# A Mamba mixer with an FP4 FFN on one core: state tiles of four states by 32 channels with quadrant sums, tanh silu, preparation a turn ahead, delta*x through two DRAM buffers

## The reference

```
xs, z = split(x @ in_w)                       # 512 channels each
xc    = silu(cb + sum_k shift(xs, k) * cw[k]) # 4 taps
dt, B, C = split(xc @ xp_w)                   # 16, 16, 16
delta = softplus(dt @ dt_w + dt_b);  A = -exp(A_log)
h[t]  = h[t-1] * exp(delta[t]*A) + (delta[t]*xc[t]) * B[t]   # 512 channels x 16 states
y[t]  = sum_n h[t,:,n] * C[t,n] + xc[t] * D
x     = layer_norm((y * silu(z)) @ out_w + x)
```

## Time and profile before

| | us |
|---|---|
| median of three runs (12323.26 to 12326.33) | 12323.49 |
| the profiled execution's own time | 12305.88 |
| its span, first to last instruction | 12304.1 |
| from the first scan to the last one's end | 11013.3 |
| the same for one of 64 turns | 172.1 |

### The profile page before, as it was taken

One profiled execution on the slowest core, in us unless ns is written; L12 is line 12 of the kernel. 1 busy time (PEld: TensorE's weight loads), 2 busy tenths in 40 slices (PEclk: granted clock), 3 DMA queues, 4 the chain that ended last, 5 costly groups with the idle time before them and its releaser, 6 DMA issues. The chain is left out here.

```text
span 12304.1 us, 107024 instructions
## 1 busy us (share of the span) xinstructions
PE 8618.5 (70%) x20260; PEld 3527.3 (29%) x20260; DVE 11095.7 (90%) x14024; ACT 4922.0 (40%) x6934; POOL 7372.0 (60%) x5182
## 2 busy tenths in 40 slices
PE   4767777777777777777777777777777777775566
PEld 1222222222222222222222222222222222222344
DVE  7999999999999999999999999999999999996555
ACT  3434443444434443444444443444344443442222
...
GB/s 91 34 38 36 38 21 38 37 43 28 34 38 36 38 21 38 38 41 31 31 38 36 38 25 35 37 43 31 31 38 36 38 25 35 38 35 25 25 25 23
DMA packets 191635, 433.27 MB, mean 35 GB/s; under 512 B 10928, under 2 KB 155056, under 8 KB 157552
## 3 DMA queue, kind: packets, MB, share of 16 engines
q1 hardware_dynamic: 190960, 427.63, 9.8%
...
## 5 line engine op out<-in xcount | busy, mean ns | idle before, releaser
L632 POOL TENSOR_TENSOR hc<-h,c_all 128x512 f32<-128x512 f32 x4096 | 5833.3, 1426 | 3959.7 <-DVE h L711 2933.5
L711 DVE TENSOR_TENSOR_SCAN h<-dA,carry,bu 128x512 f32<-128x512 f32 x4032 | 5123.5, 1271 | 73.4 <-ACT dA L485 71.4
L485 ACT ACTIVATE dA<-delta,cur 128x512 f32<-128x512 f32 x4096 | 2866.1, 719 | 5566.7 <-DVE h L711 5436.8
L361 PE MATMUL acc<-hc,ident 128*128 128x512 f32 x8192 | 4988.2, 695 | 3.2 <-POOL hc L632 3.0
L351 PE MATMUL B_all<-bsp,sel 128*128 128x512 bf16 x4096 | 1809.0, 442 | 2851.1 <-DVE bu L699 2829.1
L699 DVE TENSOR_TENSOR bu<-du,B_all 128x512 f32<-128x512 f32 x4096 | 2825.9, 690 | 521.6 <-PE B_all L351 276.3
L351 PEld LDWEIGHTS B_all<-bsp,sel 128*128 128x128 bf16 x4096 | 412.1, 101 | 5960.9 <-DVE bu L699 5663.9
L361 PEld LDWEIGHTS acc<-hc,ident 128*128 128x128 f32 x8192 | 1830.6, 225 | 542.9 <-issue 304.7
L391 PE MATMUL work<-xT,inw 128*128 128x512 f32 x2048 | 1065.7, 647 | 1.4 <-DMA dtw<-in_dtw 1.4
L764 DVE SCALAR_TENSOR_TENSOR xc<-xs,cur,xc 128x512 f32<-128x512 f32 x768 | 786.3, 1024 | 0.4
L718 DVE TENSOR_SCALAR carry<-h,keep 128x4 f32<-128x4 f32 x1023 | 625.6, 612 | 2.0
...
## 6 DMA issues: line engine op xcount, KB each, us to landing
c_all<-c_dram SPq DMA_DIRECT2D x256, 1024.0 KB, 4.7
x_in<-xbuf SPq DMA_DIRECT2D x64, 512.0 KB, 6.0
x_res<-xbuf SPq DMA_DIRECT2D x64, 512.0 KB, 6.5
xbuf<-x_res SPq DMA_DIRECT2D x64, 512.0 KB, 2.9
n_x<-in_x SPq DMA_DIRECT2D x18, 512.0 KB, 3.4
f_xa<-in_x SPq DMA_DIRECT2D x17, 512.0 KB, 4.1
f_xm<-xbuf SPq DMA_DIRECT2D x17, 512.0 KB, 5.0
xbuf<-n_x SPq DMA_DIRECT2D x16, 512.0 KB, 2.9
```

Of the source, the lines that this page charges most:

```text
L361: pe.matmul(acc[q % 2][:], ident[:], hc[:, s % RING_HC, :], start=s == 0, stop=s == NS - 1, skip_group_check=True).then_inc(summed, 1)
L485: act.activation(dA[:, s % RING_DA, :], delta[:, p_, q, :], ACT.Exp, scale=cur[:, p_, C_A + NS * q + s:C_A + NS * q + s + 1]).then_inc(da_ ...
L632: pool.tensor_tensor(hc[:, s % RING_HC, :], h[:, s % RING_H, :], c_all[:, s, :], ALU.mult).then_inc(hc_ready, 1)
L711: dve.tensor_tensor_scan(h[:, s % RING_H, :], dA[:, s % RING_DA, :], bu[s % RING_BU][:], start, ALU.mult, ALU.add).then_inc(scanned, 1)
```

## The change

A turn now has 16 **groups** s (quarter q = s // 4 of the channels, j = s % 4) in place of 64 units. A tile of a group has four states on its 128 partitions (32 rows each) for 32 channels; a group has four such tiles k, for 128 channels in all. So one spread of B (32-bit, one bank `B_all`) serves the whole group, and a DVE or POOL instruction takes two tiles (1024 columns). For this delta and delta*x must lie four times over: `store_delta` and `store_du` write them to DRAM (a buffer for each, two chunks deep) and `replicate` reads each quarter back four times into `drep` and `durep`. The sum over states is a product with `gather` (128 x 32) into a quadrant of 32 partitions of `acc`, four to a group, on top of D*x, which is a product of its own (`skip_term`). The convolution's taps are products with diagonal matrices on PE (`convolve`); `keep_states`, the carried columns and the normalising go to ACT; the cubic of softplus goes to ACT and POOL; the residual is added by PE in `project_out`. The projection in, and three of four blocks' taps, are made two turns ahead. Four turns stand in a loop body. The normalising of the input and the FFN are as before.

The diff, cut to its core (removed lines are left out; they can be seen in the kernel above):

```diff
+                for k in range(4):
+                    sp.dma_start(crep[32 * k:32 * k + 32, j, :],
+                                 c_dram[p_, 4 * j + k].partition_broadcast(32)).then_inc(c_loaded[j], 16)
+
+            def replicate(dst, src, q, done):
+                rows = src[P * q:P * q + P].rearrange("(g r) t -> r g t", r=32)
+                for k in range(4):
+                    sp.dma_start(dst[32 * k:32 * k + 32], rows).then_inc(done, 16)
...
+            def load_du(n, p_, q):
+
+                if q >= 2:
+                    sp.wait_ge(bu_ready, 2 * NG * n + 8 * (q - 2) + 8)
+                elif q == 0:
+                    sp.wait_ge(du_stored, 16 * (n + 1))
+                elif positive(n):
+                    sp.wait_ge(bu_ready, 2 * NG * n)
+                replicate(durep[q % 2], du_dram[p_], q, du_loaded[q % 2])
...
+            def store_du(n, p_):
+                sp.wait_ge(du_ready, n + 1)
+                sp.dma_start(du_dram[p_].rearrange("(e p) t -> p e t", p=P), relu[:]).then_inc(du_stored, 16)
...
+            def broadcast_b(at, p_):
                 if at is None:
                     return
+                n, s, G = at
+                if positive(G):
+                    pe.wait_ge(bu_ready, 2 * G)
+                pe.matmul(B_all[:], spread_b[:, s % QS, :], dtc[:, p_, :], start=True, stop=True).then_inc(bb_ready, 1)
+
+            def skip_term(n, p_, q):
+                if q == 0:
+                    pe.wait_ge(skip_w, 16 * layer_of(n) + 16)
+                if positive(DB * n + q):
+                    pe.wait_ge(acc_read, DB * n + q)
+                pe.matmul(acc[:], skip[:, q, :], xc[:, p_, q, :], start=True, stop=False, skip_group_check=True)
+
...
+            def sum_states(at, p_):
...
+                if s % QS == 0:
+                    skip_term(n, p_, s // QS)
+                for k in range(4):
+                    if k % 2 == 0:
+                        pe.wait_ge(hc_ready, 2 * G + k // 2 + 1)
+                    ins = pe.matmul(acc[32 * k:32 * k + 32, :], gather[:], hc[:, 4 * (s % 2) + k, :], start=False,
+                                    stop=s % QS == QS - 1, skip_group_check=True)
+                    if k % 2 == 1:
+                        ins.then_inc(summed, 1)
+
...
+            def convolve(n, e):
+                b = e % 2
+                if e == 0:
+                    pe.wait_ge(mid_w, 48 * layer_of(n) + 48)
+                wait_free(pe, b, fill(b, n, f"c{e}"))
+                for k in range(4):
+                    ins = pe.matmul(W[b][:], taps[:, 4 * e + k, :], xs[:, e, k:k + T], start=k == 0, stop=k == 3)
+                ins.then_inc(w_filled[b], 1)
 
...
+            def turn(g, ph):
+                here = ph % 2
+                nxt, other = g + 1, 1 - here
+                for s in range(NG):
+                    broadcast_b(group(g, s + 1), here if s + 1 < NG else other)
...
+                    sum_states(group(g, s - 2), here if s >= 2 else other)
                     if not is_last(g):
+                        if s == 0:
+                            convolve(nxt, 3)
+                        if s == 2:
+                            project_x(nxt, other)
+                        if s in (3, 4):
+                            project_dt(nxt, other, 2 * (s - 3))
+                            project_dt(nxt, other, 2 * (s - 3) + 1)
                     if not is_first(g):
+                        if s in (5, 6):
+                            project_out(g - 1, other, s - 5)
                     if not is_last(g):
+                        if s in (8, 9):
+                            project_in(nxt, 2 * (s - 8), 1)
+                            project_in(nxt, 2 * (s - 8) + 1, 1)
+                        if not (isinstance(g, int) and g == TOT - 2):
+                            if s == 10:
+                                transpose_x(g + 2)
+                            if s in (11, 12):
+                                project_in(g + 2, 2 * (s - 11), 0)
+                                project_in(g + 2, 2 * (s - 11) + 1, 0)
+                            if s in (13, 14, 15):
+                                convolve(g + 2, s - 13)
 
...
+            def keep_states(at):
+                if at is None:
+                    return
+                n, s, G = at
+                act.wait_ge(scanned, 4 * G + 4)
+                r = 4 * (s % 2)
+                act.copy(carry[:, 4 * s:4 * s + 4], h[:, r:r + 4, T - 1]).then_inc(carried, 1)
+
...
+            def sigmoids(n):
                 act.preload_act_table_set(SIGMOID)
+                act.wait_ge(w_read[0], fill(0, n, "dt3") + 1)
+                act.wait_ge(w_read[1], fill(1, n, "dt2") + 1)
+                act.activation(za[:], za[:], ACT.Sigmoid, bias=minus_ln2[:, 0:1], scale=-1.0).then_inc(z_of_dt, 1)
                 act.wait_ge(z_of_dt, n + 1)
+                act.activation(lin, za[:], ACT.Square).then_inc(zz_ready, 1)
+                act.preload_act_table_set(EXP_LN)
+
+            def polynomial(n):
                 act.wait_ge(zz_ready, n + 1)
...
+            def turn(g, ph):
+                here = ph % 2
+                n, other = g + 1, 1 - here
+                for s in range(NG):
+                    keep_states(group(g, s - 1))
+                    exp(group(g, s + 1), here if s + 1 < NG else other)
                     if not is_last(g):
...
+                        if s == 0:
+                            copy_conv(n, other, 2)
+                            take_params(n, other)
+                        if s == 1:
+                            copy_conv(n, other, 3)
+                            tanh_xc(n, other)
+                    if s == 1:
+                        if is_last(g):
+                            act.preload_act_table_set(SILU_TANH)
+                        silu_z(g, here)
+                        act.preload_act_table_set(EXP_LN)
+                    if not is_last(g):
+                        if s == 3:
+                            copy_proj(n, other)
+                        if s in (4, 5):
+                            delta_linear(n, other, 2 * (s - 4))
+                            delta_linear(n, other, 2 * (s - 4) + 1)
+                        if s == 5:
+                            sigmoids(n)
+                        if s == 6:
+                            polynomial(n)
                     if not is_first(g):
+                        if s in (6, 7):
+                            copy_out(g - 1, s - 6)
...
+            def times_c(at):
+                n, s, G = at
+                j = s % QS
+                if s < QS:
+                    pool.wait_ge(c_loaded[j], 64 * (n + 1))
+                r = 4 * (s % 2)
+                for k in range(2):
+                    pool.wait_ge(scanned, 4 * G + 2 * k + 2)
+                    if positive(2 * G + k - 3):
+                        pool.wait_ge(summed, 2 * G + k - 3)
+                    pair = slice(r + 2 * k, r + 2 * k + 2)
+                    pool.tensor_tensor(hc[:, pair, :], h[:, pair, :], crep[:, j:j + 1, :].to_broadcast([P, 2, T]),
+                                       ALU.mult).then_inc(hc_ready, 1)
+
...
+            def softplus(n, p_, k):
 
                 if k == 0:
+                    pool.wait_ge(lin_ready, n + 1)
+                    pool.wait_ge(quad_done, n + 1)
+                    pool.tensor_tensor(quad[:], quad[:], lin, ALU.mult).then_inc(cubic, 1)
+                elif k == 1:
+                    pool.wait_ge(cubic, n + 1)
+                    pool.tensor_tensor(quad[:], quad[:], za[:], ALU.mult).then_inc(log_ready, 1)
+                elif k == 2:
+                    pool.wait_ge(log_ready, n + 1)
+                    pool.tensor_tensor(za[:], quad[:], relu[:], ALU.add).then_inc(delta_ready, 1)
+                else:
+                    pool.wait_ge(delta_ready, n + 1)
+                    pool.wait_ge(xc_ready, n + 1)
+                    pool.tensor_tensor(relu[:], za[:], xc[:, p_], ALU.mult).then_inc(du_ready, 1)
...
+            def turn(g, ph):
+                other = 1 - ph % 2
+                for s in range(NG):
                     if not is_last(g):
+                        if s == 2:
+                            silu_xc(g + 1, other)
+                        if s == 7:
+                            softplus(g + 1, other, 0)
+                    times_c(group(g, s))
                     if not is_first(g):
+                        if s == 10:
+                            variance(g - 1)
+                        if s == 12:
+                            newton_step(g - 1)
+                    if not is_last(g):
+                        if s == 8:
+                            softplus(g + 1, other, 1)
+                        if s in (10, 11):
+                            softplus(g + 1, other, s - 8)
+                    if not is_first(g):
+                        if s == 15:
+                            affine(g - 1, 0)
+                            affine(g - 1, 1)
+
...
```

(41 more changed lines are left out.)

1012 lines of the change are left out of this document (475 added, 537 removed).

## The result

The changed kernel takes **8877.2 us** at the median (8869.2 to 8879.3, 4 runs); the kernel before took 12324.9 us beside it. The ratio is 0.720, 95% interval 0.7188 to 0.7212.

What follows compares the result with a forecast made beforehand. DVE was taken as the bound: 117.2 us a turn plus 10.8 of waits gives 128. 64 turns, 1290.8 us outside and 34 of first preparation make 9516.8, plus 19.4 gives 9540 us; range 9000 to 10900.

Steps and rivals of the forecast that it cites:

- the 19.4 us from span to median: Whole kernel: 19.4 us added to the summed span of 9516.8 us to give the forecast time.
- The bound: Turns: DVE bounds the kernel, with short waits for PE; POOL's and ACT's idle time follows DVE's scan.
- DVE's floor: DVE's turn: scans, bu, gates and statistics from start to start sum to 117.2 us, against 172.1 a turn before.
- What the new coupling costs: DVE's waits in a turn, with one bank of B_all, ACT's bursts and a longer PE queue: 9% of 117.2, 10.8 us.
- The trip of delta*x: Way through DRAM: delta*x ready at 98 us, store and read end by 108, bu needs it at 114.8; cover 7 us.
- the lower bound: PE's 64 sums a turn: four quadrants side by side, 13.7 us, PE in all 75.5; about 34 was taken.
- Rival (a): PE's sums not overlapped at all, not even loads: PE bounds, T = 138 to 153, 10200 to 11140 us; chance 13%.
- POOL and ACT: Work per turn: POOL 104 us, 89% of DVE's floor; ACT 82 us, not the bound but in bursts.
- No new waits for inputs in SBUF: New DVE instructions: each reads one operand from SBUF, as scan and bu do now, so no such waits were charged.
- The list of what goes: DVE's turn: taps 12.3 us, carry 9.8, carried columns 4.8, cubic, parts of B, silu, normalising and some 10 us idle go.
- The first preparation: Before the first scan: POOL steps 22.5 us, DRAM trip 10 and PE's taps, less DVE's taps: +34 us, bounds 15 and 60.
- The floor is reached: Rival (c), turns: DVE runs at its floor, T = 118 to 120 us, 8900 to 9025 us in all; chance 5%.

Runs made afterwards that it cites:

- half_bu: The changed kernel with half of every bu left out, the second scan of a pair reading the first one's half again; 8721 us.
- one_quadrant: The changed kernel with all four sums of a group going to the first 32 rows of acc instead of four quadrants; 9438 us.

## Why the prediction was wrong, step by step

The error against the profiled span is 9516.8 - 8877.4 = 639 us: 64 x (128 - 117.7) = 658 too much in the turns, 18 too little outside. With the 19.4 us from span to median, which were 0 here, and the rounding to 9540 that is the 663.

- **The bound: right, but with little room.** DVE is at work for 114.7 of 117.7 us a turn, and no experiment with less work for ACT or POOL in the changed kernel gained over 11 us. But with 16.3 us less work for DVE (half_bu) T fell by 2.5 only: the chains through POOL, ACT and PE stand close behind, which the prediction, with POOL at 89% and ACT at 70% of DVE's floor, didn't see.
- **What the new coupling costs, 10.8 us a turn: wrong, 496 us.** It was 3.05. The 9% was the old share of waits nearly doubled, and no row stood behind it. The reasons given don't hold: with two quadrants the sums take 1.84 us a group, near the 2.1 that I assumed, and the time rises by 8 us. One bank of B_all with 2.4 us of room is enough as long as a group's work on PE (5.5 us here, 6.3 there) is shorter than DVE's 7.0. The granted clock did not keep its 0.85 but rose with PE's work (below).
- **Of those 3.05 us, 2.1 were two things, one named and one missed.** The trip of delta*x was named with a cover of 7 us and had none, 0.7 us a turn: POOL's last product ends 98 us into the turn, as forecast (97 in the turn shown above), but store and loads took 16.5 us in that turn, not 10 (its traffic took 42.4% of 16 engines' span for 903 MB, 4.2 us a MB, where the earlier trace rows gave 2.8). The loop's jump, 5.3 to 6.7 us of DVE's time every fourth turn and 1.3 us a turn on the mean, was missed.
- **DVE's floor, 117.2 us: 2.5 too high, 160 us.** The terms: a scan 1.18 us from start to start, not 1.19; a bu 1.12, not 1.14 (recorded 1212 ns, forecast 1.20). Missed was that a quarter of the turns scan from zero, without a carry: 3.36 for 3.48 us, 32 times, 3.8 us in each, 1 us on the mean.
- **PE: the lower bound was right.** Sums of 34 us a turn were assumed near the upper end, because it had the only row; they take 16. Rival (a) was right that serial sums make PE the bound, but its T of 138 to 153 (134 to 151 by its own terms, 61.8 + 16 x 4.5 to 5.6) was 124 to 126: a pair of records takes 0.86 to 0.89 us in a row, not 1.02, and no load is added. By the rule of the Trainium skill (TensorE: Matmul & The Clock Gate, Packing small matmuls — row/col tiling, The mechanism) that a load overlaps running products only when the row group differs, the group would be, by an estimate from this case's records, 8 x (0.43 + 0.11) = 4.3 us; one_quadrant, whose products all have the same rows, shows 3.55, so the rule doesn't hold here.
- **POOL and ACT: right in total** (102.5 for 104, 78.6 for 82; products 2361 and 4530 ns for 2.34 and 4.49), **wrong in use.** I read POOL's 104 of 117 as 13 us of room. In groups 3 to 7 there is such room, in the rest of the turn hardly any: 4.7 us of work in groups 13 and 14 cost 3.5.
- **No new waits for inputs in SBUF: right,** and worth more than I made of it. The list of what goes took the carry at 9.8 us a turn. Kept on DVE beside POOL's longer instructions it would have cost 18.6.
- **The first preparation,** +34 (15 to 60): +48.5, from 164.20 to 212.67 at the first scan; the end is 5.2 us longer.
- **The range.** "The floor is reached" had 5% and 8900 to 9025 us; even that lay too high, since the floor was. The other chances all rested on waits that no row priced.
